# Edge tiles filled by destination in a graph attention layer: 202 steps of exchange for 208, spill and score stores placed tile by tile

## What is computed

```python
K, Q, V = typed_linear(x, Wk, bk), typed_linear(x, Wq, bq), typed_linear(x, Wv, bv)   # [6250, 192] each, by node_type
e0, e1, e2 = cos(log(edge_attr[:, 0..2] + 1) * w_time + b_time)                        # [200000, 32] each
row, col = src, dst
att   = einsum('ehd,ed->eh', cat(K[row], e1) as 4 heads of 56, sum of heads of cat(Q[col], e2)) / sqrt(56)
att_i = the same with row and col, e1 and e2 exchanged
att, att_i = softmax of att over the edges with one col, of att_i over those with one row
agg = segment_sum(cat(v * att, e0), col) + segment_sum(cat(v_i * att_i, e0), row)      # [6250, 256]
o = typed_linear(cat(agg, agg), Wa, ba);  y = layernorm(o + x) * gamma[type] + beta[type]
out = layernorm(x + y)
```

## Time and profile before

| | us |
|---|---|
| median of three runs | 8200.95 |
| fastest, slowest run | 8191.16, 8206.43 |
| the profiled execution, time | 8195.39 |
| its span | 8193.7 |
| PE busy | 5584.1 (68%) |
| weight loads (PEld) | 4015.8 (49%) |
| DVE busy | 6340.5 (77%) |
| ACT busy | 4450.3 (54%) |
| POOL busy | 5776.4 (70%) |
| mean granted TensorE clock | 0.807 |
| moved by DMA | 1936 MB, 236 GB/s |

### The profile page before, as it was taken

How to read it: one execution, slowest core, us unless ns; L and a number is a source line. 1 busy time by engine, 2 the same in 40 slices (tenths; PEclk the granted TensorE clock), 3 DMA queues, 4 the chain that set the end, 5 groups by cost and what they waited for, 6 DMA issues and landing times. The chain is left out here.

```text
span 8193.7 us, 133450 instructions
## 1 busy us (share of the span) xinstructions
PE 5584.1 (68%) x34300; PEld 4015.8 (49%) x34301; DVE 6340.5 (77%) x9003; ACT 4450.3 (54%) x12726; POOL 5776.4 (70%) x6077
## 2 busy tenths in 40 slices
PE   7767777767676667676766666732777774299966
PEld 6456666666663333333333333322555553288854
DVE  8378888888887888888888888855666664588877
ACT  0134444444445666666666666633666663288845
POOL 3657777777776777777777777747777775188856
PEclk5866666676767888888888888866999997699987
DMA  2554453343336888888988888885999999899973
GB/s 78 187 179 131 129 150 114 111 130 109 117 111 197 300 292 298 299 296 293 301 295 295 299 292 300 298 201 212 393 389 389 388 388 211 62 286 288 287 244 114
DMA packets 1549522, 1936.30 MB, mean 236 GB/s; under 512 B 429993, under 2 KB 1354899, under 8 KB 1549083
## 3 DMA queue, kind: packets, MB, share of 16 engines
q1 hardware_dynamic: 1060126, 1029.14, 40.3%
q0 software_dynamic: 255392, 674.52, 26.0%
q10 hardware_dynamic: 233824, 230.96, 8.3%
HBM read 1090.09 MB, written 872.85 MB: 240 GB/s over the span
## 5 line engine op out<-in xcount | busy, mean ns | idle before, releaser
L1195 PE MATMUL exch_pG<-far_tab,exch_ohT 128*128 x3328 | 1593.2, 630 | 671.0 <-ACT exch_kc L1112 667.6
L1055 POOL DMA_INDIRECT exch_row<-table,exch_of x1664 | 1590.3, 956 | 553.0 <-issue 513.1
L1571 PE MATMUL sum_pS<-sum_row,sum_oh 128*128 128x260 f32 x6656 | 1625.0, 403 | 441.3 <-DVE edge_acc L1621 339.5
L940 POOL DMA_INDIRECT recs<-place_rec,place_addr x1568 | 1504.3, 959 | 583.6 <-issue 547.3
L1571 PEld LDWEIGHTS sum_pS<-sum_row,sum_oh 128*128 128x128 f32 x6656 | 1292.5, 199 | 773.4 <-DVE edge_acc L1621 413.3
L1195 PEld LDWEIGHTS exch_pG<-far_tab,exch_ohT 128*128 128x128 f32 x3328 | 728.7, 226 | 1484.4 <-issue 1445.6
L1269 POOL DMA_INDIRECT bys<-sum_pb x960 | 940.7, 980 | 314.2 <-issue 280.8
L1589 ACT ACTIVATE sum_off<-kept_ramp,sum_neg 128x128 f32<-128x128 f32 x3120 | 953.5, 387 | 99.8 <-POOL sum_neg L1526 99.8
L1111 ACT ACTIVATE exch_pb<-exch_pG 128x192 f32<-128x192 f32 x1664 | 555.6, 334 | 422.6 <-PE exch_pG L1195 346.5
L1269 POOL DMA_INDIRECT bys<-exch_pb x624 | 620.8, 995 | 215.6 <-issue 188.0
L1611 DVE TENSOR_TENSOR sum_row<-sum_row,sum_pF 128x1792 f32<-128x1792 f32 x208 | 420.3, 2021 | 355.4 <-DMA sum_row<-spill 353.4
(11 more groups left out here) (324 smaller groups left out, 11996.0 us busy)
## 6 DMA issues: line engine op xcount, KB each, us to landing
bys<-place_none SPq DMA_DIRECT2D x52, 4224.0 KB
spill<-exch_row SPq DMA_DIRECT2D x208, 1024.0 KB, 9.8
sum_row<-bys SPq DMA_DIRECT2D x208, 1024.0 KB
sum_row<-spill ACTq DMA_DIRECT2D x206, 1024.0 KB
mid<-exch_pb SPq DMA_DIRECT2D x208, 660.0 KB
sum_pb<-mid SPq DMA_DIRECT2D x192, 660.0 KB
exch_row<-table,exch_of POOLq DMA_INDIRECT x1664
recs<-place_rec,place_addr POOLq DMA_INDIRECT x1568
```

Source lines behind the costliest of these rows:

```text
L940: nc.gpsimd.indirect_dma_start(recs, bass.IndirectOffsetOnAxis(addr[:, par, t:t + 1], 0), rec[:, par, t, :], None).then_inc(s_scat[par], 16)
L1055: nc.gpsimd.indirect_dma_start(row[q][:, t, TD:TD + S.TW], None, table, bass.IndirectOffsetOnAxis(of[q][:, t:t + 1], 0)).then_inc(s_row[q] ...
L1195: nc.tensor.matmul(pG[t % 3][:, 0:GW], ohT[ring(j, 2)][:, t, :], flat[:, bass.ds(tiles[t] * GW, GW)], start=True, stop=True).then_inc(s_ga ...
L1571: last = nc.tensor.matmul(pS[j % SETS * HG + t // 2][:, 0:AW], oh[h][:, t, :], row[j][:, t, :], start=(t % 2 == 0), stop=(t % 2 == 1))
```

## The change

**Tiles.** Direction 0 fills whole tiles by owner, no longer pairs, so 1616 tiles hold it (NTD) and the exchange has 202 steps. Direction 1 is as it was. Aggregate 0 still works by pairs with 208 steps: so each tile of the exchange has a place of its own in the order by pairs, `where[t]`, its number plus the shifts of the owners before it. The table `k.table` has [33, NT] integers, the tile's owner in row 0 and its place in row 32. An owner with an odd number of tiles leaves its last place empty; SP blanks `spill` and `runs` there.

**Place.** `pairs` (DVE, 13 operations in project) gives the paired starts, the shift of each owner and its last place. `owners_of_tiles` is done three times (whole tiles into `k.table`, pairs of direction 0 into `otile0`, direction 1), with bf16 factors and 33 output rows.

**Exchange.** SP loads 8 registers and stores `spill` with 8 DMAs, each to its place. `runs` goes from SP to ScalarE's queue: `scores`, at the end of ACT's step, loads 8 registers and issues 8 DMAs. The ring of `at` has three buffers. `mid` stays in the order of the exchange.

**Softmax 0 and aggregate 0.** AHEAD 16 becomes 18, EARLY 8 becomes 6; aggregate 0 forwards 184 steps. The table of tiles by pairs is loaded in softmax 0 from `otile0`.

**Output.** Direction 1's denominators, divisions and sum go into the output's DVE program, in two halves of the owners (25 and 24); SP stores each half when it is done. `W` is queued before the wait for the stores.

```diff
 class Sizes:
+        self.NTD = -(-((self.E + self.NO * (P - 1)) // P) // (2 * self.G)) * 2 * self.G
-        self.AHEAD = 16
-        self.EARLY = 8
+        self.AHEAD = 18
+        self.EARLY = 6
 def starts(...):
-    link(nc.vector.tensor_scalar(sti[:], st[:, 4, :], float(2 * P - 1), None, ALU.add))
-    link(nc.vector.tensor_scalar(sti[:], sti[:], 8, None, ALU.logical_shift_right))
-    link(nc.vector.tensor_scalar(st[:, 1, :], sti[:], 2.0, None, ALU.mult))
+    link(nc.vector.tensor_scalar(sti[:], st[:, 4, :], float(whole * P - 1), None, ALU.add))
+    link(nc.vector.tensor_scalar(sti[:], sti[:], 6 + whole, None, ALU.logical_shift_right))
+    link(nc.vector.tensor_scalar(st[:, 1, :], sti[:], float(whole), None, ALU.mult))
+def pairs(nc, k, link, st, of, sti, zero, junk, c):
+    tot, begin = of[:, 4, :], of[:, 3, :]
+    NO = tot.shape[1]
+    link(nc.vector.tensor_scalar(sti[:], tot, float(2 * P - 1), None, ALU.add))
+    link(nc.vector.tensor_scalar(sti[:], sti[:], 8, None, ALU.logical_shift_right))
+    link(nc.vector.tensor_scalar(st[:, 0, :], sti[:], 2.0, None, ALU.mult))
+    link(nc.vector.tensor_tensor_scan(st[:, 1, :], st[:, 0, :], zero[:, 0:NO], 0.0, ALU.add, ALU.add))
...
+    nc.vector.tensor_scalar(c.last[:], st[:, 1, :], -1.0, 0.0, ALU.add, ALU.max)
...
+    for row, to in ((2, c.stq), (4, c.shift)):
+        link(nc.vector.tensor_tensor(junk[:], st[:, row, :], k.ident[:, 0:NO], ALU.mult))
+        link(nc.vector.tensor_reduce(to[:, 0:1], junk[:], op=ALU.add, axis=AX))
 def place_edges(...):   # SP
+            def blank(o):
+                _, (end,) = nc.values_load_multi_w_load_instructions(c.last[0:1, o:o + 1], ...)
+                sp.dma_start(spill[:, bass.ds(end, 1), :], bc(SPILT, 1, 1)).then_inc(s_blank, 16)
+                sp.dma_start(runs[:, bass.ds(end, 1), :], bc(SCORED, 1, 1)).then_inc(s_blank, 16)
...
+                if 0 <= g - 3 < NO:
+                    blank(g - 3)
...
+            sp.dma_start(spill[:, S.NTD:NT, :], bc(SPILT, 1, NT - S.NTD)).then_inc(s_blank, 16)
+            sp.dma_start(runs[:, S.NTD:NT, :], bc(SCORED, 1, NT - S.NTD)).then_inc(s_blank, 16)
             sp.wait_ge(s_first, 1)
+            sp.dma_start(otile0, otilep[:]).then_inc(s_store, 16)
 def place_edges(...):   # PE, then DVE, then POOL
-                    last = nc.tensor.matmul(to[0:1, 0:w], k.ones[0:NO, 0:1], flat[:, n * TC:n * TC + w], start=True, stop=True)
+                    last = nc.tensor.matmul(to[0:33, 0:w], sel[0:NO, :], flat[:, n * TC:n * TC + w], start=True, stop=True)
-            owners_of_tiles(0, c.stc, k.otile[0][:])
+            dve.wait_ge(s_init, 2)
+            owners_of_tiles(0, c.stc, k.table[:])
+            owners_of_tiles(1, c.stq, otilep[:]).then_inc(s_first, 1)
+            nc.gpsimd.memset(k.table[:], -1).then_inc(s_init, 1)
+            pool.wait_ge(s_init, 1)
+            nc.gpsimd.iota(k.table[32:33, :], pattern=[[1, NT]], base=0, channel_multiplier=0).then_inc(s_init, 1)
 def exchange(...):
-    NS = NT // G
+    NS = S.NTD // G
-        at = [s.sb(f"at{n}", [P, G, H + 1]) for n in range(2)]
+        at = [s.sb(f"at{n}", [P, G, H + 1]) for n in range(R)]
 # SP's step
+                _, where = nc.values_load_multi_w_load_instructions(
+                    k.where[0:1, bass.ds(n * G, G)], engines=[nc.sync.engine], ...)
                 sp.wait_ge(s_sinv, n + 1)
-                sp.dma_start(spill[:, bass.ds(n * G, G), :], row[q][:, :, 0:2 * TD + PROJ]).then_inc(s_v[q], 16)
-                sp.wait_ge(s_att, n + 1)
-                sp.dma_start(runs[:, bass.ds(n * G, G), :], at[h][:]).then_inc(s_as[h], 16)
+                for t in range(G):
+                    sp.dma_start(spill[:, bass.ds(where[t], 1), :], row[q][:, t:t + 1, 0:2 * TD + PROJ]).then_inc(s_v[q], 16)
                 sp.wait_ge(s_sco, n + 1)
                 sp.dma_start(mid[...], pb[q][:, NOW:G, :]).then_inc(s_mid[q], 16)
 # ACT
+            def scores(n, j):
+                _, where = nc.values_load_multi_w_load_instructions(
+                    k.where[0:1, bass.ds(n * G, G)], engines=[nc.scalar.engine], ...)
+                act.wait_ge(s_att, n + 1)
+                for t in range(G):
+                    nc.scalar.dma_start(runs[:, bass.ds(where[t], 1), :], at[ring(j, R)][:, t:t + 1, :]).then_inc(s_as[ring(j, R)], 16)
...
                     cosines(n + 1, i, j + 1)
                     queries(n + 1, j + 1)
+                scores(n, j)
 def aggregate(...):
-    SKIP = S.AHEAD if bys is not None else 0
+    TURNS = (S.NTD // G - S.AHEAD) // 4
+    SKIP = S.AHEAD
...
+        if d == 0:       # den, reciprocal, division; for d == 1 they are in output, with the sum
 def output(...):   # SP
-                sp.dma_start(joint[0:(NO - 1) * P, 0:OUT].rearrange("(o p) f -> p o f", p=P), t[:, 0:NO - 1, 0:OUT]).then_inc(s_o, 16)
+            for n, (a, b) in enumerate(shares):
+                sp.wait_ge(s_sum, n + 1)
+                whole = min(b, NO - 1)
+                if whole > a:
+                    sp.dma_start(joint[a * P:whole * P, 0:OUT].rearrange("(o p) f -> p o f", p=P), t[:, a:whole, 0:OUT]).then_inc(s_o, 16)
             sp.dma_start(joint[(NO - 1) * P:N, 0:OUT], t[0:S.LAST, NO - 1, 0:OUT]).then_inc(s_o, 16)
-            sp.wait_ge(s_o, STORED)
             for c in range(OC):
                 sp.dma_start(W[:, c], wsum[...]).then_inc(s_w, 16)
+            sp.wait_ge(s_o, STORED)
```

More of the change, by code:

```diff
@@ L666, in _ @@
             sp.wait_ge(s_none, 2)
+            SPILT, SCORED = none[:, 0:S.VW], none[:, S.SC:S.SC + S.H + 1]
+            def blank(o):
+                _, (end,) = nc.values_load_multi_w_load_instructions(
+                    c.last[0:1, o:o + 1], engines=[nc.sync.engine], min_val=0, max_val=NT - 1,
+                    skip_runtime_bounds_check_because="an owner's last tile")
+                sp.dma_start(spill[:, bass.ds(end, 1), :], bc(SPILT, 1, 1)).then_inc(s_blank, 16)
+                sp.dma_start(runs[:, bass.ds(end, 1), :], bc(SCORED, 1, 1)).then_inc(s_blank, 16)
+            assert NO <= NG - 3
             part = 0
@@ L808, in _ @@
             owners_of_tiles(0)
+            owners_of_tiles(1)
             pe.wait_ge(s_tot, 1)
@@ L1541, in _ @@
         if bys is not None:
[L1542 removed]
+            with sp.Fori(0, TURNS) as i:
                 for j in range(4):
@@ L1631, in _ @@
         dve.wait_ge(s_add, NS * HG + SETS * HG)
-        link, _ = chain(dve, s_den)
-        sums = total[:].rearrange("p (o f) -> p o f", f=AW)
-        link(nc.vector.tensor_scalar(den[:], sums[:, :, VW:AW], 1e-16, None, ALU.add))
-        link(nc.vector.reciprocal(den[:], den[:]))
-        for h in range(H):
-            part = sums[:, :, head + h * DK:head + (h + 1) * DK]
-            last = nc.vector.tensor_tensor(part, part, bc(den[:, :, h], 2, DK), ALU.mult)
-        if d:
-            link(last)
-            e0 = 0 if head else H * DK
-            old = k.acc0[:].rearrange("p (o f) -> p o f", f=AW)
-            for a, b, w in ((head, k.head0, H * DK), (e0, 0 if k.head0 else H * DK, VW - H * DK)):
-                nc.vector.tensor_tensor(sums[:, :, a:a + w], sums[:, :, a:a + w], old[:, :, b:b + w], ALU.add)
+        if d == 0:
+            link, _ = chain(dve, s_den)
+            sums = total[:].rearrange("p (o f) -> p o f", f=AW)
+            link(nc.vector.tensor_scalar(den[:], sums[:, :, VW:AW], 1e-16, None, ALU.add))
+            link(nc.vector.reciprocal(den[:], den[:]))
+            for h in range(H):
+                part = sums[:, :, head + h * DK:head + (h + 1) * DK]
+                nc.vector.tensor_tensor(part, part, bc(den[:, :, h], 2, DK), ALU.mult)
 def output(nc, k, S, sums, free, W, wsum, joint, ba, gamma, beta, out):
@@ L1687, in output @@
         block = ctx.enter_context(nc.Block())
-        STORED = 32 if NO > 1 else 16
+        half = (NO + 1) // 2
+        assert NO > 2
+        shares = [(0, half), (half, NO)]
+        STORED = 16 * 3
+        den = s.sb("den", [P, NO, S.H])
+        s_sum = s.sem("sum")
+        old = k.acc0[:].rearrange("p (o f) -> p o f", f=AW)
         @block.sync
@@ L1797, in _ @@
             nc.vector.memset(eps[:], LN_EPS).then_inc(s_eps, 1)
+            H, DK, VW = S.H, S.DK, S.VW
+            link(nc.vector.tensor_scalar(den[:], t[:, :, VW:AW], 1e-16, None, ALU.add))
+            link(nc.vector.reciprocal(den[:], den[:]))
+            for a, b in shares:
+                for h in range(H):
+                    part_h = t[:, a:b, h * DK:(h + 1) * DK]
+                    last = nc.vector.tensor_tensor(part_h, part_h, bc(den[:, a:b, h], 2, DK), ALU.mult)
+                link(last)
+                for to, of, w in ((0, k.head0, H * DK), (H * DK, 0 if k.head0 else H * DK, VW - H * DK)):
+                    last = nc.vector.tensor_tensor(t[:, a:b, to:to + w], t[:, a:b, to:to + w], old[:, a:b, of:of + w], ALU.add)
+                last.then_inc(s_sum, 1)
             nc.vector.memset(ones3[:], 1.0)
@@ L1909, in gnn_resnorm @@
```

(2 more changed lines are left out.)

92 lines of the change are left out of this document (59 added, 33 removed).

## The result

The changed kernel took 8134.9 us (median of four runs, 8130.7 to 8143.6) against 8200.3 us: a ratio of 0.9925, 95% interval 0.9909 to 0.9941, so 0.8% faster, 65 us. The forecast was 8108 in a range of 8050 to 8280. The profiled execution took 8130.7 us, its span is 8129.0 against 8193.7.

A forecast was written before the change was run, and what follows sets the result against it. POOL, issuing 11 DMAs in 13.94 us a step, was taken to bound the exchange. Exchange -42, softmax 0 +12.8, aggregate 0 -49 and output -12 sum to -90 on 8195.4: 8105, given as 8108, range 8050 to 8280.

The forecast's parts named there:

- Project and place: Stages before the exchange: small DVE operations, table setup and blank stores hide in existing waits, so no cost.
- third round of owners_of_tiles: End of place: with bf16 factors three rounds take 19 to 23 us against 21, so nothing; +10.5 if bf16 gives nothing.
- The exchange: 202 steps of 14.15 us, set by the ACT-DVE loop with the score stores, gain 42 us of a possible 84.
- Rival A: Exchange: POOL remains the bound and the new stores fit entirely, 13.94 us a step, total 8063; chance 0.25.
- Rival B: Exchange: ScalarE's stores stand on its path, making the kernel slower than before, from 8215 us upward; chance 0.20.
- Rival C: Exchange: small writes fill the DMA engines; at 50 ns a row 15.5 us a step, total 8380; chance 0.05.
- Rival D: Exchange: SP and ACT bursts exclude each other, each ACT store waits one of SP, 16.8 us a step, 8640; chance 0.03.
- Softmax 0: Softmax of direction 0: 18 steps go ahead instead of 16, so 90 forwards instead of 80, +12.8 us.
- aggregate 0: Aggregation of direction 0: 40 fewer POOL forwards, -51.1, last ones sooner, -6.6, read-back beside row loads, +8; net -49 us.
- output: Final stage: sums stored in two halves, stored 10.7 us earlier, W queued already; -12 us in all (0 to -20).
- beta's landing: Output stage, a sign that the forecast is right: beta lands 39 us after the last sum.
- signs of B: Exchange, marks that would show Rival B: ACT stores over 0.4 us each, POOL waiting over 1 us a step for DVE.

The follow-up runs named there:

- the one with the stores moved: Changed kernel with each step's eight score stores issued one after each tile's two copies in ScalarE's next gathered part: 8084.5 us, ratio 0.9853 to the kernel before.
- the run with twelve: Changed kernel with four more score stores a step on ScalarE's queue, behind the eight, into a spare DRAM place: 8702.1 us, ratio 1.0610 to the kernel before.

## Why the prediction was right, and where it was not

**The sum.** Forecast -90, profiled -64.7, inside the range. (5.6 on 8105 would be 8111, not the 8108 given.) The missing 25 us are one term, "Project and place ... the blank stores are SP's, which waited most of the stage" (+28.2 where it stood at nothing; the other terms together came out 3 better). That sentence looked at who issues the stores, not at what they put into the DMA engines. The other 98 blank stores move one row a partition each; the two at the end move 48 tiles at once. Spreading these two takes 22.7 of the 28.2 us back. Of the rest, 1.3 are there at the first scatter and some 4 more before the last groups, while the other blanks go out; no run tests those. The third round of owners_of_tiles cost nothing, as forecast: with bf16 factors DVE waits 1.7 us for PE in a round where it waited 5.8. I had costed these DMAs at nothing because their queue waits, and had not named who needs the same DMA engines: the scatters of the records. ACT's reuse of the records' buffer waits for their landing, and behind it stood DVE, 21.9 us, and POOL, 15.9.

**The exchange.** Forecast -42, profiled -43.6, and by the mechanism named: the loop L1102, DVE's scores, the queue, L1102. The parts against the forecast's: 8.75 for 8.76; 1.10 for 0.2 + 0.8; 4.00 for 8 x 0.52 = 4.16; 0.53 for 0.2. The turn of the loop was not in my sum (5.5 us at 15 turns, 0.4 a step) and the stores were a little cheaper (median pitch 0.494). That the gain came out within 2 us is in part luck: the step was forecast at 14.15 and took 14.36, and I took 13.94 a step for the kernel before, whose trace gives 14.15 over the whole stage, its turns and its start included; both sides were short by the same 0.2. Rival A (POOL stays the bound) fell for this kernel and describes the one with the stores moved. Rival B was near: at the 0.557 us that a store took in the run with twelve, eight would take 0.46 us a step more, an estimate of 92 us in all, which is more than the whole gain.

**DMA engines and exclusion.** From 2600 to 5400 us 199,955 rows of 20 bytes on ACT's queue took 8.9 ns each by the packet records, under the 10 ns I took from the read-back; in the 294 us of the earlier trace rows the share went from 0.88 to 0.94. The Trainium skill, DMA: Bandwidth & Descriptors (Specifications), has transfers under 512 bytes as read-modify-write. The exchange's rows show no price for it; the blank's, 92 ns each, show a price, but no run says that it is this one. Rival C (small writes fill the DMA engines) was the right effect at the wrong place. As to SP and ACT, the forecast's count of 0 held, but its reading of the earlier trace rows did not. SP's issue there (a load, not a store) starts at 6001.02, ACT's ends at 6001.10: they share 0.08 us, so "within" is wrong and the row decides nothing. The changed kernel shows more. Of its 58 ACT stores over 0.4 us, 51 overlapped an issue or load of SP, and of the 1558 short ones 392. Beside a spill store of SP 17 of 25 were long, elsewhere 41 of 1591. All the excess is 33 us in 1616 stores, not all of it on the path. With the stores between the evictions, 1064 of 1616 go out beside a spill store; 187 of these are long, and 62 of the other 552. So the two queues do lengthen each other's issues at times. But in 353 pairs of that run an ACT store and a spill store share over 0.2 us and neither takes over 0.4. The Trainium skill (Perfetto Trace Analysis, DMA Instruction, HWDGE) has the descriptor generator locked for exclusive use; these pairs do not look like a lock that is held for a whole issue. Rival D fell: eight spill stores or one made no difference.

**Softmax 0, aggregate 0, output.** +14.4 for +12.8, -48.4 for -49. The forwards of aggregate 0 took 57.9 us less, and I had 51.1 + 6.6; the read-back grew by 10.0 us beside the last row loads, and I had 8. The read-back begins 57.0 us sooner after the last forward of softmax 0, where "some 57" stood. Output -14.2 for -12, with the halves worth 8.8 where I had 10.7, and W's order nothing beside them. One mark was wrong: the prediction has beta's landing 39 us after the last sum; DVE's use of it came 51 us after it (7933.67 against 7882.5), and 13.5 us sooner after the first denominator than the earlier trace rows show, which is what the sum needed.

**The marks.** L1328 ran 202 times; the landing wait at ACT is gone; from the end of the scores to the next L1165 it is 5.6 us for the 5.3 given (5.2 within a round); POOL's waits for DVE are short, 71.6 us in 82 times. Of the signs of B, the stores' length stays away too: their median issue is 0.338 us.

## What to carry to other kernels

A store issued from a compute engine's queue costs its issue, 0.5 us each here, where that queue's next instruction closes the loop that bounds the kernel; between instructions that wait for another engine anyway, the same stores cost nothing that this kernel's step shows (14.10 us, before the change 14.15). Before a DMA is costed at nothing because its queue is idle, count its rows: 6144 small pieces in one DMA filled all engines for over 20 us here, and what suffered was a landing somewhere else. When two engines are within a few per cent of each other, read both kernels' step from the same marks, loop turns included.

## What the runs showed of the hardware

- One DMA of 6144 pieces of 20 bytes that lie side by side in DRAM (48 in a row for each of 128 partitions, all from one 20-byte source per partition) kept the 16 DMA engines busy for over 20 us: 92 ns a piece, with a median of 9. Rows of 20 bytes, 128 to a DMA and 33 KB apart, took 8.9 ns. As 128 rows of 960 bytes the blank delayed the first gather no longer (2530.6 us, and 2531.5 with it spread). Whether it is that the pieces are neighbours, that they share a source or that so many stand in one DMA was not separated.
- The turn of ACT's unrolled loop of 12 steps takes 5.5 us (mean of 15) from the last store to the next operation, where it is 0.13 within the loop. In the kernel before, where POOL was the bound, the step across the turn took 16.4 us on average beside a median of 13.6, and the round as a whole only what POOL needs; once ACT's queue is in the bounding loop, the step takes 19.1 beside 13.6.
- Issues of SP and ACT that overlap are longer at times: in the kernel with the stores between the evictions 187 of 1064 ACT stores beside a spill store took over 0.4 us, where the median is 0.34.
- SP's load of eight registers took 1.95 us (median of 202, the shortest 0.52), ACT's 0.55 of the same table. Why they differ was not tried. Here SP's was hidden.
